# Four stacked graph layers on one core: first stage by groups of blocks, node numbers and spike state in PSUM, 64 early scatters

## The chip, the cores and the metric

The program runs on one core of one Trainium2 chip. The metric is the device time of one execution in microseconds (us). Engines are named as in the profile: PE is TensorE (PEld its weight loads), DVE is VectorE, ACT is ScalarE, POOL is GpSimd, SP is SyncE, which only issues DMAs here. A node graph of 6250 nodes, padded to 49 blocks of 128, has 106250 edges, padded to 832 tiles of 128.

## The reference

```python
x = x + L0(relu(layernorm(x)))      # x: [6250, 128]
x = x + L1(relu(layernorm(x)))
x = x + L2(relu(layernorm(x)))
x = x + L3(relu(layernorm(x)))
# L0, hyperbolic: two Moebius steps (product with weight.T, addition of a fixed bias
#   point), log map, sum over edges src->dst, exp map, relu of the log map, exp map
def mobius_add(x, y):
    x2, y2, xy = sum(x*x), sum(y*y), sum(x*y)
    return ((1 + 2*xy + y2)*x + (1 - x2)*y) / max(1 + 2*xy + x2*y2, MIN_NORM)
# L1, graph attention with 4 heads (softmax over a node's edges), then 25 steps of
def step(mem):                       # a spiking neuron on every element of h
    mem = 0.9*mem + h
    spk = mem > 1.0
    return mem - spk, spk            # result: spikes / 25
# L2: for each of 4 edge types, sums over edges in both directions, times matrices
# L3: two graph convolutions with edge weights, layer norms between
```

## The kernel before

All of x, and most of what is made from it, stays in SBUF as 49 blocks of 128 nodes (`X`, `H`, `T`, `ACC`, 128 x 6272 and a little more). `GB = 7` blocks are a group, `NG = 7` groups are all.

**A walk** sums over edges. The rows of the source nodes lie in a table in DRAM. POOL runs through the 832 tiles of edges and issues one indirect DMA for each (L619): it gathers the table's rows for 128 edges into `GATHERED`. Four tiles are a chunk, 208 chunks are a walk, and `GATHERED` is a ring of four chunks. For each chunk DVE makes a one-hot matrix of destinations: `IOTA` (the numbers of a block's 128 nodes, int16) compared with a column of destinations, `DSTF` (L1309, 128 x 512, a `tensor_tensor` with `is_equal`), PE multiplies it with the gathered rows (L730), and DVE adds the product to the block's sum (L1332). Chunks that touch a second block do this again. DVE then frees the chunk's place in the ring (L1371, a semaphore that POOL waits for). There are six such passes over the edges with gathers: l0, g1 (attention; without one-hots on DVE), l2, l2b, l3a, l3b. l3a and l3b make their one-hots as four `tensor_scalar` instructions with weights (L1315). A seventh pass, gb, reads back by SP's DMAs what g1 has gathered.

**Beside walk l0** DVE sorts the edges by source block. In the first half `count` compares `BUCKET` with a number (L1488, `SAME`) and adds up (L1497), in the second `rank` does for 50 buckets: `SAME` (L1488), a scan `BEFORE` over `ONE` and `SAME` (L1535), `BEFORE * SAME` (L1538), `PLACEF + BEFORE` (L1540). All lie in `EX` in SBUF, 832 columns each. The places are used by 832 **scatters** (L632, indirect DMAs of POOL into `list_dram`): `EARLY = 96` of them after walk l0, the next 336 after walk g1, and the last 400 after gb. POOL's queue is in this order: walk l0, 96 scatters, wait for the stored table `gat_tab`, walk g1, 336 scatters, wait for the end of gb, 400 scatters, wait for the stored `typed_tab`, walk l2, walk l2b, l3a, l3b.

**Before walk l0** (the first stage) SP loads everything, with x near the end; DVE waits for all 39 loads (L1138), turns the edge lists into columns, makes the weights ready, and then works on all 49 blocks at once: layer norm, a dense product group by group (`dense`, `copy_dense`), and the formulas of L0 as 128 x 6272 passes with small 128 x 49 computations between. DVE asks ACT for square roots, logarithms and so on (`ask`), and waits for each answer. One DMA stores `T` as `row_tab0` (L512), and POOL's walk waits for it.

**After walk l0** the rest of L0 is done in the same manner, and then a layer norm by groups: `norm_groups` runs `center`, `variance` and `normed` of DVE for group after group, shifted against each other by one step, while ACT squares and PE multiplies, and SP stores `gat_tab` in seven pieces (`store_groups("l1", ...)`, `n_out`).

**The spikes** (L1766 to L1787): for each group 25 steps on 128 x 896 elements in two halves. DVE computes `MEM = -0.9 * NEG + cur` (L1776) and `NEG = (MEM > 1) - MEM` (L1780), each as two instructions of 448 columns, all in SBUF; ACT makes spikes of `MEM` (L1074, L1045), PE adds them up in PSUM. `typed_beside` does layer 2's norm and products for the group before between the steps.

The kernel's instructions are all written in one function, `program`.

Of the kernel before, what the change touches and what calls it, by code (L numbers as in the profile page):

```python
# [28 lines left out]
F32 = mybir.dt.float32  # L29
# [7 lines left out]
P = 128  # L37
# [25 lines left out]
def program(nc, x, src, dst, etype, weight, w0, b0, w1, att_src, att_dst, b1,  # L63
# [37 lines left out]
    EARLY = 6 * BATCH  # L101
    MIDDLE = EARLY + 21 * BATCH
# [18 lines left out]
    with ctx:  # L121
# [34 lines left out]
        DST2 = SM[:, 0:NT]  # L156
# [19 lines left out]
        W0T = sb("W0T", [P, D])  # L176
# [14 lines left out]
        RI = T[0:RP, 0:3 * RK * P].bitcast(I32)  # L191
        RF = H[0:RP, 0:4 * RK * P]
        RSZ = RK * P
        R16 = H[0:RP, 4 * RK * P:5 * RK * P].bitcast(I16)
        SAME, BEFORE, PLACEF, BUCKET = (EX[:, k * NT:(k + 1) * NT] for k in range(4))
# [12 lines left out]
        WLIN = T[:, 3 * RSZ:3 * RSZ + 2 * NT4 * D]  # L208
        W0N = EQ[:, 3 * D:4 * D]
        RANGEF = T[0:1, 4 * RSZ:4 * RSZ + 4 * NCH]  # L210

        s_in = sem("s_in")
        s_pad = sem("s_pad")
# [71 lines left out]
        class Dense:  # L285
            def __init__(self, n, product=True):
                self.stage = sem(f"dense_stage_{n}")
                self.tr = sem(f"dense_tr_{n}")
                if product:
                    self.ht = sem(f"dense_ht_{n}")  # L290
                    self.mm = sem(f"dense_mm_{n}")
                self.out = sem(f"dense_out_{n}")
# [7 lines left out]
        denses = {"l0": 0}  # L300
        norms = {n: k for k, n in enumerate(("l1", "l2", "l3a", "l3b", "out"))}
# [4 lines left out]
        N_LOADS = 39  # L306
# [59 lines left out]

        def small(k):
            return SM[:, k * NB:(k + 1) * NB]

        STAGE = G[:, 0:GB * D]  # L370
# [41 lines left out]
        def runs_bank(h):  # L412
# [6 lines left out]
        NEG = ACC[:, 2 * GB * D:3 * GB * D]  # L419
# [3 lines left out]
        TURNED, NODE_TERM = (PS[:, 1024 * k:1024 * k + GB * D] for k in (1, 2))  # L423
# [3 lines left out]
        SQ_T = (H[:, 0:NB * D], T[:, 0:NB * D], ACT.Square)  # L427
        requests = {
            "before_l0": [SQ_T,
                          (small(0), small(1), ACT.Sqrt),  # L430
                          (T[:, 0:NB * D], H[:, 0:NB * D], ACT.Square),
                          (small(2), small(3), ACT.Sqrt),
                          (SMALL[:, 41:42], SMALL[:, 40:41], ACT.Sqrt),
                          (SMALL[:, 43:44], SMALL[:, 42:43], ACT.Tanh)],
            "l0": [(H[:, 0:NB * D], T[:, 0:NB * D], ACT.Square),
# [21 lines left out]
        def _(sp):  # L457
# [4 lines left out]
            def load(dst_, src_):  # L462
                sp.dma_start(dst_, src_).then_inc(s_in, 16)
# [1390 lines left out]
```

## Time and profile before

| | us |
|---|---|
| three runs | 8385.81, 8386.53, 8389.94 |
| median | 8386.53 |
| the profiled execution | 8386.38 |
| its span in the trace | 8384.7 |
| DVE busy | 3407.2 (41%) |
| PE busy | 3380.2 (40%) |
| POOL busy | 5866.1 (70%) |
| ACT busy | 1148.5 (14%) |

The span is the time from the first to the last instruction in the trace; the profiled execution lasted 1.7 us longer than it. The prediction's sum is made against 8386.4. In rows of a timeline the first number is the start in us, the second the duration, and `x2` says that two instructions are merged; a row's bracket has the idle time before it and what ended it.

### The profile page before, as it was taken

Reading aid. Unit: us, or ns where it says so; the run is one execution under the profiler, and the core shown is the slowest. Engines: PE = TensorE matmul, PEld = TensorE weight load, DVE = VectorE, ACT = ScalarE, POOL = GpSimd, SP = SyncE. Lnnn points to the kernel's source line nnn. Section 1 sums busy time; section 2 is a strip of 40 time slices with the busy share of each in tenths; the row PEclk is TensorE's granted clock in tenths of the full one; section 3 lists DMA queues with packets and bytes.
Section 4 is the critical chain, followed back from the end, with each engine's and each line's share of the span. In section 5 each row is a group of like instructions: output and inputs, shape, how many; then the busy total and the mean of one; then the engine's idle time right before and its main releaser. Section 6 shows DMA issues by size and latency. Waiting matters only on the chain.

```text
span 8384.7 us, 80823 instructions
## 1 busy us (share of the span) xinstructions
PE 3380.2 (40%) x13790; PEld 2554.1 (30%) x13791; DVE 3407.2 (41%) x7346; ACT 1148.5 (14%) x1948; POOL 5866.1 (70%) x5837
## 2 busy tenths in 40 slices
PE   1344443100002665442555543333345544455553
PEld 1244332100002555111444431111134444344442
DVE  4434656300004556992323323333343333433335
ACT  1000001333331111772000000000010000100001
POOL 0577777777777751787777777777757777477774
PEclk7555555555555666565555555555555555555555
DMA  1112111355553332001222222222222121111111
GB/s 39 52 51 50 45 46 33 92 135 135 135 135 84 87 86 67 19 27 39 70 70 70 69 65 77 77 76 77 76 54 52 52 53 52 48 52 53 52 52 47
DMA packets 348608, 555.47 MB, mean 66 GB/s; under 512 B 121171, under 2 KB 200871, under 8 KB 348511
## 3 DMA queue, kind: packets, MB, share of 16 engines
q0 software_dynamic: 199680, 357.35, 17.7%
q1 hardware_dynamic: 148831, 197.20, 7.8%
q14 instruction: 82, 0.67, 0.0%
q8 instruction: 15, 0.25, 0.0%
HBM read 448.57 MB, written 105.56 MB: 66 GB/s over the span
## 4 chain that ended last, share of the span: by engine, by line
POOL 41%; issue 21%; PE 16%; DVE 10%; DMA 7%; DVEq 4%; ACT 1%; SPq 0%; ACTq 0%; POOLq 0%
POOL GATHERED L619 34%; PE PS L730 15%; POOL list_dram L632 7%; DVE OH L1315 2%; DMA GATHERED<-row_tab,SRCI 2%; DMA GATHERED<-typed_b_tab,PLACE 2%; DVEq L317 1%; DVE OH L1309 1%; DMA GATHERED<-gat_tab,SRCI 1%; DVE T L1120 1%; DVE SM L1130 1%; DMA gat_rows<-GATHERED 1%; DMA GATHERED<-typed_tab,KEYF 1%; DVEq L319 1%; DVE T L1705 1%
## 5 line engine op out<-in xcount | busy, mean ns | idle before, releaser
L730 PE MATMUL PS<-GATHERED,OH 128*128 128x128 f32 (+2 forms) x9216 | 2434.1, 441 | 3059.1 <-DVE OH L1309 688.3
L619 POOL DMA_INDIRECT GATHERED<-row_tab,SRCI x2496 | 2466.4, 988 | 1157.8 <-issue 688.1
L730 PEld LDWEIGHTS PS<-GATHERED,OH 128*128 128x128 f32 (+1 forms) x9216 | 1899.7, 300 | 3651.7 <-issue 2182.7
L632 POOL DMA_INDIRECT list_dram<-REC,PLACE x832 | 973.8, 1170 | 507.7 <-issue 261.5
L619 POOL DMA_INDIRECT GATHERED<-typed_b_tab,PLACE x832 | 816.0, 981 | 261.7 <-issue 224.8
L619 POOL DMA_INDIRECT GATHERED<-typed_tab,KEYF x832 | 818.1, 983 | 253.6 <-issue 241.1
L619 POOL DMA_INDIRECT GATHERED<-gat_tab,SRCI x832 | 785.0, 943 | 253.6 <-issue 222.8
L1315 DVE TENSOR_SCALAR OH<-IOTA,DSTF,WF 128x128 f32 x2048 | 581.5, 360 | 433.3 <-issue 406.9
L1332 DVE TENSOR_TENSOR T<-T,PS 128x128 f32 x512 | 146.8, 287 | 962.7 <-PE PS L730 961.2
L730 PE MATMUL PS<-T,OH 128*128 128x132 f32 x2048 | 426.6, 382 | 241.2 <-DVE OH L1309 141.1
L730 PEld LDWEIGHTS PS<-T,OH 128*128 128x128 f32 x2048 | 383.1, 280 | 284.7 <-issue 193.2
L787 PE MATMUL PS<-AMP,EQ 128*128 x832 | 60.3, 177 | 977.4 <-DVE EX L1622 962.5
L1309 DVE TENSOR_TENSOR OH<-IOTA,DSTF 128x512 f32 (+1 forms) x512 | 353.8, 691 | 136.4 <-issue 123.4
L1332 DVE TENSOR_TENSOR ACC<-ACC,PS 128x129 f32 (+1 forms) x512 | 147.9, 289 | 624.4 <-PE PS L730 623.6
L1332 DVE TENSOR_TENSOR X<-X,PS 128x128 f32 x256 | 73.7, 288 | 714.0 <-PE PS L730 713.8
L787 PEld LDWEIGHTS PS<-AMP,EQ 128*128 128x128 bf16 x832 | 38.4, 107 | 998.6 <-issue 998.6
L928 ACT ACTIVATE H<-T,DINV 128x128 f32<-128x128 f32 x98 | 29.9, 394 | 2103.7 <-DVEq L1825 2103.7
L1622 DVE TENSOR_REDUCE EX<-PS 128x48 f32 x208 | 43.2, 208 | 674.3 <-DMA gat_rows<-GATHERED 489.9
L1335 DVE TENSOR_REDUCE EQ<-PS 128x128 f32<-128x384 f32 x256 | 142.7, 557 | 425.0 <-PE PS L730 425.0
L1309 DVE TENSOR_TENSOR OH<-IOTA,REC 128x512 bf16 (+1 forms) x256 | 177.7, 694 | 215.2 <-issue 213.1
L866 PE MATMUL PS<-ACC,WSB 128*128 128x448 bf16 x350 | 145.0, 514 | 283.1 <-ACT ACC L1045 283.1
L1002 ACT ACTIVATE SCR<-ROWI,SM 128x512 bf16<-128x512 int16 x208 | 150.0, 721 | 670.8 <-DMA ROWI<-dst_rows 667.8
(268 smaller groups left out, 3415.0 us busy)
## 6 DMA issues: line engine op xcount, KB each, us to landing
gat_rows<-GATHERED SPq DMA_DIRECT2D x208, 264.0 KB, 2.3
GATHERED<-gat_rows SPq DMA_DIRECT2D x208, 264.0 KB
GATHERED<-row_tab,SRCI POOLq DMA_INDIRECT x2496, 2.5
ROWI<-dst_rows SPq DMA_DIRECT2D x208, 128.0 KB
typed_b_tab<-ACC SPq DMA_DIRECT2D x49, 384.0 KB, 2.4
list_dram<-REC,PLACE POOLq DMA_INDIRECT x832
GATHERED<-gat_tab,SRCI POOLq DMA_INDIRECT x832
GATHERED<-typed_tab,KEYF POOLq DMA_INDIRECT x832, 2.5
```

The costliest lines, as they stand in the source:

```text
L317: eng.load(regs[p], table[0:1, bass.ds(c * REGS, REGS)])
L319: eng.reg_alu(counts[p][k], regs[p][k], 0, ALU.max)
L619: pool.indirect_dma_start(out=rows_at[:, u * CT + t, 0:width], out_offset=None, in_=table, in_offset=bass.IndirectOffsetOnAxis(ap=rows[:, ...
L632: pool.indirect_dma_start(out=list_dram, out_offset=bass.IndirectOffsetOnAxis(ap=PLACE[:, t:t + 1], axis=0), in_=REC[:, 2 * t:2 * t + 2], ...
L730: last = mm(bank(p)[:, 0:r.shape[1]], onehot(p, t, 1, onehots_), r, start=(t == 0), stop=(t == CT - 1))
L787: last = mm(bank(k)[:, t * AW:(t + 1) * AW], onehots_[:, t * P:(t + 1) * P], AMP[:, bass.ds(b * AW, AW)], start=True, stop=True)
L866: last = mm(SPIKES[:, k, :], IDB, SPK[t % 2][:, k * (GB * D // 2):(k + 1) * (GB * D // 2)], start=(t == 0), stop=(t == LIF_T - 1))
L1002: nc.scalar.activation(SCRB[:, CE:2 * CE], ROWI[:, u * CE:(u + 1) * CE], ACT.Abs, bias=NODE[:, bass.ds(first, 1)], scale=float(FAR)).then_ ...
L1309: return v.tensor_tensor(onehot(p, 0, CT, of).rearrange("p (t w) -> p t w", t=CT), IOTA[:, bass.ds(b * P, P)].rearrange("p (o w) -> p o w" ...
L1315: last = v.tensor_scalar(onehot(p, t), IOTA[:, bass.ds(b * P, P)], DSTF[:, bass.ds(c * CT + t, 1)], weights[:, bass.ds(c * CT + t, 1)], AL ...
L1332: return v.tensor_tensor(dest, dest, bank(p)[:, 0:F], ALU.add)
L1335: return v.tensor_reduce(JOINED[k], bank(p)[:, 0:NP3 * F].rearrange("p (i f) -> p f i", i=NP3), axis=AX.X, op=ALU.add)
```

## The change

1. **First stage by groups.** W0, the bias b0 and x are loaded first, x in two parts (blocks 0 to 20, then the rest), each with its own semaphore. The norm and the product of L0 run through `norm_groups("l0", ...)` with a fourth part, `squared`, five steps late. ACT takes the products out of PSUM, and their squares. The product gets a 129th column, `W0T` times the bias point, so that the dot products with the bias come from PE; the norms of the input rows come from PE too (`HN2`). The length of the Moebius sum is worked out from the small numbers instead of by passes over all blocks. Edge lists, chunk ends and weights are made ready between the small computations (`post()` in place of `ask()`, `answered()` later), some of it on ACT. `T` is finished and stored in seven groups; ACT makes the 49 blocks of bias rows. The zeroing of `ACC` moves to POOL.
2. **Node numbers in PSUM.** The column that one-hots are compared with is now `COLUMN`, in PSUM, copied there for each walk; `SAME` and `PLACEF` are in PSUM too.
3. **64 early scatters** instead of 96; 368 after g1 instead of 336; the last 400 as before.
4. **Spikes.** `NEG` is in PSUM. The `memset` and the first step's `MEM` are left out (the first membrane value is `cur`), and the last step's `NEG`.

```diff
-    EARLY = 6 * BATCH
-    MIDDLE = EARLY + 21 * BATCH
+    EARLY = 4 * BATCH
+    MIDDLE = EARLY + 23 * BATCH
-        SAME, BEFORE, PLACEF, BUCKET = (EX[:, k * NT:(k + 1) * NT] for k in range(4))
+        BLOCK_OF, BEFORE, BUCKET = (EX[:, k * NT:(k + 1) * NT] for k in range(3))
+        PLACEF, COLUMN, SAME = (PS[:, 1024 * k:1024 * k + NT] for k in (1, 2, 3))
-        NEG = ACC[:, 2 * GB * D:3 * GB * D]
+        NEG = [PS[:, 2048 + 512 * h:2048 + 512 * h + HALF] for h in range(2)]
...
@@ SP
+            load(W0N, w0, s_first)
+            bcast(YROW, b0.rearrange("a b -> (a b)"), s_first)
+            for k, b0_ in enumerate(X_PARTS):                       # X_PARTS = (0, 3)
+                a, b = b0_ * GB, (X_PARTS[k + 1] * GB if k + 1 < len(X_PARTS) else NB - 1)
+                load(X3[:, a:b, :], x[a * P:b * P, :].rearrange("(b p) f -> p b f", p=P), s_x[k])
...
-            sp.dma_start(row_tabs[0].rearrange("(b p) f -> p b f", p=P), T3).then_inc(s_stored, 16)
+            for g in range(NG):
+                sp.wait_ge(s_tab, g + 1)
+                sp.dma_start(row_tabs[0][g * GB * P:(g + 1) * GB * P, :].rearrange("(b p) f -> p b f", p=P),
+                             group(T3, g)).then_inc(s_stored, 16)
@@ POOL
+            pool.wait_ge(s_pair, 1)
+            pool.wait_ge(s_wt, 3)
+            pool.memset(ACC[:, :], 0.0).then_inc(s_zero, 1)
-            pool.wait_ge(s_stored, 16)
+            pool.wait_ge(s_stored, 16 * NG)
             walk("l0", row_tabs[0], D, SRCI)
@@ ACT
+            def product_rows(g):
+                columns_out(g, D + 1, 0, D, T3, ACT.Copy)
+                columns_out(g, D + 1, 0, D, H3, ACT.Square)
+                return columns_out(g, D + 1, D, D + 1, small(20).rearrange("p (b o) -> p b o", o=1), ACT.Copy)
+            norm_groups("l0", product_rows, squares=True)
...
+            act.wait_ge(s_h, 2)
+            for g in range(NG):
+                for b in range(g * GB, (g + 1) * GB):
+                    last = nc.scalar.activation(H3[:, b, :], YROW, ACT.Copy, scale=small(22)[:, b:b + 1])
+                last.then_inc(n_biased, 1)
@@ DVE
+            norm_groups("l0", X3, arrivals=X_PARTS, squares=5)
+            post()
+            edge_rows()
+            answered()
+            dve.sem_inc(s_rows, 1)
+            post()
+            ts(small(2), small(2), MIN_NORM, None, ALU.max)
+            chunk_ends()
+            answered()
...
-            tt(H3, T3, over(YROW, NB), ALU.mult)
-            total(xy, H3)
...
-            tt(T3, T3, spread(small(21)), ALU.mult)
-            tt(H3, over(YROW, NB), spread(small(22)), ALU.mult)
-            tt(T3, T3, H3, ALU.add)
-            ask()
-            total(small(5), H3)
-            ask()
+            (seven 128 x 49 operations)
+            post()
+            source_blocks()
+            answered()
...
+            dve.sem_inc(s_h, 1)
+            for g in range(NG):
+                tt(group(T3, g), group(T3, g), spread(group_of(21, g)), ALU.mult)
+                dve.wait_ge(n_biased, g + 1)
+                tt(group(T3, g), group(T3, g), group(H3, g), ALU.add)
+                dve.sem_inc(s_tab, 1)
...
-                                           column[:, bass.ds(c * CT, CT)]...
+                                           COLUMN[:, bass.ds(c * CT, CT)]...
...
-                v.memset(NEG, 0.0).then_inc(lif, 1)
                 for t in range(LIF_T):
+                    mem = MEM[t % 2] if t else cur
+                    if t:
+                        (two MEM halves, from NEG[h] in PSUM and half(cur, h))
+                    if t < LIF_T - 1:
+                        (two NEG halves, out=NEG[h] in PSUM, in0=half(mem, h), in1=half(mem, h))
```

The lines in round brackets stand for instructions told above.

## Rows read from the trace of the kernel before

**Rows 1.** The chain of work that ended last, its shares by engine.
```profile
POOL 41%; issue 21%; PE 16%; DVE 10%; DMA 7%; DVEq 4%; ACT 1%; SPq 0%; ACTq 0%; POOLq 0%
```

**Rows 2.** Busy time by stage: window, its length, engines' busy time (instructions), PE clock, DMA share, GB/s.
```profile
0.00:265.90 265.90, 40.77 (x245) 37.82 (x246) 145.92 (x168) 46.40 (x36) 6.92 (x14) 0.67 0.17 43
265.90:1409.60 1143.70, 525.64 (x2044) 457.25 (x2044) 575.60 (x855) 43.22 (x207) 889.28 (x832) 0.50 0.18 48
1409.60:1559.90 150.30, 27.17 (x169) 23.77 (x167) 93.92 (x117) 47.13 (x72) 120.74 (x98) 0.59 0.12 29
1559.90:2598.40 1038.50, 72.56 (x1012) 46.66 (x1012) 99.01 (x510) 363.46 (x504) 784.97 (x832) 0.50 0.56 134
2598.40:3320.10 721.70, 439.69 (x2118) 394.04 (x2118) 434.36 (x769) 111.24 (x260) 369.49 (x336) 0.67 0.30 79
3320.10:3929.90 609.80, 219.92 (x595) 76.87 (x595) 466.89 (x795) 364.26 (x422) 483.63 (x400) 0.60 0.08 22
3929.90:5001.40 1071.50, 574.71 (x2187) 451.63 (x2187) 316.81 (x607) 83.27 (x195) 818.07 (x832) 0.57 0.25 70
5001.40:6079.10 1077.70, 374.07 (x1028) 112.22 (x1028) 395.20 (x768) 0.00 (x0) 815.96 (x832) 0.50 0.28 76
6079.10:7176.50 1097.40, 543.61 (x2191) 468.81 (x2191) 396.50 (x1331) 26.38 (x70) 787.89 (x832) 0.55 0.20 53
```

**Rows 3.** Timeline of walk l0 in its second half, DVE and POOL.
```profile
1005.95 0.65 DVE L1488 TENSOR_SCALAR EX<-EX,KCOL 128x832 f32<-128x832 f32 x1 [0.24 <-issue]
1006.75 1.95 DVE L1535 TENSOR_TENSOR_SCAN EX<-ONE,H,EX 128x832 f32<-128x832 f32 x1
1007.03 2.42 POOL L619 DMA_INDIRECT GATHERED<-row_tab,SRCI  x1 [0.30 <-issue]
1009.76 0.94 POOL L619 DMA_INDIRECT GATHERED<-row_tab,SRCI  x1 [0.30 <-issue]
```

**Rows 4.** Timeline of the spikes.
```profile
3349.45 1.30 POOL L632 DMA_INDIRECT list_dram<-REC,PLACE  x1 [0.30 <-issue]
...
3350.90 1.15 DVE L1776 SCALAR_TENSOR_TENSOR ACC<-ACC,T 128x448 f32<-128x448 f32 x2
3351.06 1.30 POOL L632 DMA_INDIRECT list_dram<-REC,PLACE  x1 [0.31 <-issue]
```

**Rows 5.** Groups of instructions, shapes apart: busy us, mean ns of one, idle before.
```profile
L1309 DVE TENSOR_TENSOR OH<-IOTA,DSTF 128x512 f32 x504 | 348.3, 691 | 131.4 <-issue 119.6
...
L1807 DVE TENSOR_TENSOR ACC<-PS,ACC 128x512 f32<-128x512 f32 x49 | 33.9, 692 | 9.3 <-issue 9.3
L928 ACT ACTIVATE H<-T,DINV 128x128 f32<-128x128 f32 x98 | 29.9, 394 | 2103.7 <-DVEq L1825 2103.7
```

**Rows 6.** Timeline after walk l0: norm by groups, the 64th scatter, and SP past the stores.
```profile
1500.76 1.09 DVE L1130 TENSOR_REDUCE SM<-X 128x7 f32<-128x896 f32 x1
...
1506.24 1.09 DVE L1130 TENSOR_REDUCE SM<-X 128x7 f32<-128x896 f32 x1
...
1511.08 1.33 POOL L632 DMA_INDIRECT list_dram<-REC,PLACE  x1 [0.30 <-issue]
...
1528.07 0.35 SPq L533 DMA_DIRECT2D ACC<-dst_rows  x1
```

**Rows 7.** Timeline of the first stage: the load of x, the table's store, the first gather.
```profile
14.60 16.14 SPq L463 DMA_DIRECT2D X<-in_x  x2
...
253.09 0.39 SPq L512 DMA_DIRECT2D row_tab<-T  x1
...
265.89 1.11 POOL L619 DMA_INDIRECT GATHERED<-row_tab,SRCI  x1 [258.32 <-DMA row_tab<-T]
```

**Rows 8.** Busy time in pieces of the first stage, columns as in rows 2.
```profile
48.60:85.00 36.40, 17.81 (x98) 17.03 (x98) 20.08 (x34) 0.00 (x0) 0.00 (x0) 0.77 0.04 6
...
178.60:188.80 10.20, 0.00 (x0) 0.00 (x0) 8.08 (x35) 3.29 (x5) 0.00 (x0) 0.50 0.00 0
...
202.20:205.20 3.00, 0.00 (x0) 0.00 (x0) 2.61 (x12) 0.00 (x0) 0.00 (x0) 0.50 0.00 0
...
238.00:246.30 8.30, 0.00 (x0) 0.00 (x0) 6.89 (x31) 1.50 (x2) 0.00 (x0) 0.50 0.00 0
```

More of the change, by code:

```diff
@@ L299, in program @@
         typed_mm = sem("typed_mm")
-        denses = {"l0": 0}
-        norms = {n: k for k, n in enumerate(("l1", "l2", "l3a", "l3b", "out"))}
+        norms = {n: k for k, n in enumerate(("l0", "l1", "l2", "l3a", "l3b", "out"))}
         stores = {"l3a": 1, "l3b": 2}
@@ new lines, in edge_columns, with columns, cols @@
+            def edge_columns():
+                def columns(a):
+                    return PS[:, 1024 * a:1024 * (a + 1)].rearrange("p (b f) -> p b f", b=2)[:, :, 0:4 * RP]
+                def cols(t):
+                    return t[:, :].rearrange("p (b f) -> p b f", b=2)
+                dve.wait_ge(s_const, 9)
+                dve.wait_ge(s_cols, 1)
+                step(v.tensor_copy(cols(SRCF), columns(0)))
+                step(v.tensor_copy(cols(DSTF), columns(1)))
+                step(v.tensor_copy(cols(KEYF), columns(2)))
+                step(v.tensor_copy(cols(WF), columns(3)))
+                dve.sem_inc(s_wc, 1)
@@ new lines, in source_blocks @@
+            def source_blocks():
+                step(v.tensor_copy(SRCI[:, :], SRCF[:, :]))
+                dve.sem_inc(walks["l0"].free, RING)
+                step(v.tensor_copy(BLOCK_OF.bitcast(I32), SRCF[:, :]))
+                step(v.tensor_single_scalar(BEFORE.bitcast(I32), BLOCK_OF.bitcast(I32), 7, ALU.logical_shift_right))
+                step(v.tensor_copy(BUCKET, BEFORE.bitcast(I32)))
+                dve.wait_ge(s_drow, 64)
+                chunk_table(RANGEF, RANGES)
+                dve.sem_inc(s_info, 1)
@@ L1266, in normed, with squared @@
                     dve.sem_inc(n_normed, 1)
-                for s in range(NG + 2):
-                    for part, g in ((center, s), (variance, s - 1), (normed, s - 2)):
-                        if 0 <= g < NG:
-                            part(g)
+                def squared(g):
+                    dve.wait_ge(n_out, k * NG + g + 1)
+                    total(small(squares)[:, g * GB:(g + 1) * GB], group(H3, g))
+                parts = [(center, 0), (variance, 1), (normed, 2)] + ([(squared, 5)] if squares else [])
+                for s in range(NG + parts[-1][1]):
+                    for part, late in parts:
+                        if 0 <= s - late < NG:
+                            part(s - late)
             def artanh(o, n):
@@ L1322, in all_added, with aggregate @@
                 hold(dve, wk.more_added, before + more + 1)
-            def aggregate(name, result, F, weights=None, ahead=None, column=DSTF, table=RANGES,
+            def aggregate(name, result, F, weights=None, ahead=None, table=RANGES,
                           parts=((NIT - 1, None, None),), sets=2, joins=False):
@@ L1699, in _ @@
             dve.sem_inc(v_made, RING)
+            step(v.tensor_copy(COLUMN, DSTF[:, :]))
             wk = walks["gb"]
@@ L1796, in _ @@
             stt(other, DSTF[:, :], 1.0, other, ALU.add, ALU.mult)
-            tt(DST2, DSTF[:, :], other, ALU.subtract)
+            tt(COLUMN, DSTF[:, :], other, ALU.subtract)
             for s in (nb_turned, nb_ht, nb_mm, nb_made, nb_high, nb_rest, nb_middle):
```

482 lines of the change are left out of this document (219 added, 263 removed).

## Prediction

> **What bounds the kernel now.** I read the chain of waits first. Its largest shares are POOL with 41% and "issue" with 21%, ahead of PE with 16% [rows 1]; "issue" is mostly the 0.30 us that lie between two of POOL's DMA instructions. Then I cut the span into stages, a window for each item of POOL's queue [rows 2]. Nine windows say what sets each stage. In a walk nothing is waited for but POOL: walk g1 takes 1038.5 us for 832 gathers, 1.248 us each, of which 784.97 / 832 = 0.943 us busy. Walk l3a, whose one-hots are made by `tensor_scalar`, keeps that busy time (787.89 / 832 = 0.947). But l0 has 889.28 / 832 = 1.069, l2 983 ns and l2b 981 ns, all for the same instruction.
>
> The timelines say why. While DVE runs the scan L1535 (1.95 us, operands `ONE` and `SAME`, both in SBUF), a gather takes 2.42 us, and the next one 0.94 [rows 3]. In the spikes, where DVE issues instructions with two SBUF tensors back to back, every scatter takes 1.30 us (0.97 elsewhere) and starts 1.61 us after the one before, three times the 0.535 us between two starts of DVE [rows 4]. So POOL waits for the DVE instruction in progress to end when that instruction reads two tensors from SBUF. I compared every POOL duration with what DVE ran beside it: instructions that read one of their two tensors from PSUM (L1332, L1807) left it at 0.94. DVE itself is not slowed, with 691 ns for every one-hot [rows 5].
>
> **The change part by part.**
>
> *Walks.* With `COLUMN` in PSUM a one-hot has one SBUF tensor; so have the scan, the product and the sum of `rank`. L1488 wrote `SAME` in SBUF in 0.65 us; into PSUM I take 1.02, the time of the other passes over 832 columns, since 0.65 is too short for a column a cycle. In a pair of chunks of the ranking half (10.0 us after the change) DVE then has some 7.6 us of work, still under POOL. Walk l0: 1143.7 - 832 x 1.249 = 104.5, less 4 for the passes half-way that still read `SRCF` and `DSTF`: **-101**. Walk l2: 1071.5 - 1040 - 5.5 for L1811, which keeps two SBUF operands: **-26**. l2b: 1077.7, of which 8.7 is the wait before it, minus 1041 and 3 for L1340: **-25**. g1, l3a, l3b: 0. The copies into `COLUMN` add 1 us each before gb and l2b: **+2**.
>
> *Price of PSUM.* L1807 reads one tensor from PSUM and takes 692 ns for 512 columns against 691 for L1309 [rows 5]: nothing added. No row shows DVE writing to PSUM or reading there with a step of zero; nearest are the same rows, so I take 0 and bound it by double time, below, as a rival. The Trainium skill (VectorE: DVE Perf Modes, section on the TRN2 errata) gives 62 cycles more for a PSUM source than for an SBUF one, an estimate of 65 ns each; in gb, where one-hots are on the path, its 256 would add 17 us. The two rows disagree with it, so the sum leaves it out.
>
> *Early scatters.* The window after walk l0 is 150.3 us long because 96 scatters are [rows 2]. The table that g1 needs was stored at 1528.07, where SP's next DMA starts, 118.5 us after the walk; the 64th scatter began at 1511.08 and was done 16 us before [rows 6]. So the store is what ends last with 64: **-32**. With 96, g1 could gain nothing from a faster norm; with 64 the cover is 16 us. The 32 moved scatters cost 32 x 1.4 = 45 us after g1, where POOL is idle for 246 of 721.7 us [rows 2]: 0.
>
> *Last 400 scatters.* This stage is POOL's: 483.63 us busy and 400 x 0.31 between them leave nothing of its 609.8, while the spikes were done at 3808 and the last typed table was under way to DRAM by 3834 [rows 2]. 400 x 1.27 would be 508; some 70 of the 100 us lie beside L1776 and L1780, the rest beside passes that stay. L1776 now reads `NEG` from PSUM; L1780 still reads `MEM` twice. Of a period of 2.14 us half is then free of waiting. I follow three scatters: one starts free, the next (1.27 later) waits 0.335 for the end of the first NEG half, the third 0.135 for the second: 0.16 on average against 0.335. **-37**. Between -10 (POOL is held by every pair anyway) and -72 (no waits left). The operations left out, 2 us a group, are hidden.
>
> *First stage*, 265.9 us now [rows 7]. New, step by step. (a) x was issued in 16.14 us for 49 blocks; 21 blocks from 3.5 on, 7 us, and 2.5 to land: DVE starts at 13, by when the bias work (5 us of small instructions, after 6) is done. (b) `norm_groups`: the same code later has a step of 5.48 us, DVE being full [rows 6]; `squared` adds 1.12, so 6.6 from the fifth step; 2.5 + 3.8 + 3 x 5.4 + 2 x 6.6 + 3.8 + 2.5 = 42 us up to the last `normed`, and 12 until the last group's transposes, product, squares and sums (8 in that later stage, and two more ACT passes): 67. (c) Small computations that stay: 10.2 + 3.0 + 8.3 = 21.5 [rows 8]. Seven new ones, 1.7. Edge and chunk work, now between them: 17.6, most of it from the piece between 48.6 and 85.0, where DVE was busy for 20.08 us [rows 8]; the copies of the weights in that piece go to ACT. 67 + 21.5 + 1.7 + 17.6 = 108. (d) Bias rows: 49 x 0.394 = 19.3 us on ACT [rows 5], longer than DVE's 15.5 beside them, and a last sum: 128.5. (e) The last group's store lands in 3 to 3.6 instead of the 12.5 of the whole table [rows 7]: 132. POOL's zeroing of `ACC` and the weights on PE and ACT lie beside (c) with little to spare. **-134**, between -110 (each hand-over and ACT's copies late, PE at its lower clock throughout) and -145.
>
> Sum: -134 - 101 - 32 - 37 - 26 - 25 + 2 = -353. From 8386.4, the profiled execution's time, that is **8033**; the median of the three runs is 0.1 higher.
>
> **The rivals.**
>
> *A. The stretch of gathers doesn't come from two SBUF operands.* Then walks and late scatters stay, and -134 - 32 + 2 give 8222. For it: nothing in the rows; it would need another reason why l3a is clean. The Trainium skill (SBUF — State Buffer, section "Who interferes with whom") says that `tensor_tensor` takes only the shared read interface and, as an inference, that making a DMA's descriptors needs the write interface, so it would not hold it up; by that rule this is the outcome. The 2.42 us gather beside the scan speaks against the rule.
>
> *B. PSUM is slow for DVE.* The only way to a slower kernel. It is one price, time per column in the changed instructions. If it doubles, a one-hot costs 0.53 more, which in gb, where DVE and PE take turns, is 256 x 0.53 = +137; a spike half costs 0.47 more, 672 of them move the spikes' end from 3811 to 4127 on the old clock, 234 beyond POOL's new end at 3893. +371 against -353: about 8404, and the point where it turns is 95% of a doubling. L1807 and L1332 show no such price.
>
> *C. The first stage gives about 100 only*, because ACT, with five passes a group, a PE at its lower clock and the weights' chain (PE, ACT, PE, ACT) fall behind DVE: 8067. For it: 12 hand-overs in (b) and (c) that I priced by busy time.
>
> *D. The spikes' scatters stay locked* to DVE's pairs: -10 in place of -37, 8060.
>
> *E. Waits vanish beside L1780 too* (one tensor read twice), and the first stage is at its best: -35 and -11 more, 7987.
>
> **How the numbers follow.** Forecast 0.60, C 0.14, D 0.10, E 0.08, A 0.05, B 0.03. The forecast's own range, with the first stage at 125 to 145 and the scatters at 25 to 50, is 8009 to 8056. The range that should hold 8 in 10 reaches past C and D together to 8090 and nearly to E, 7990. A measurement of this kernel can tell about 0.2%, 17 us, from no change. All cases but B are faster by far more: faster 0.96, same 0.01, slower 0.03.
>
> **What would show it.** First gather near 132 us; walk l0 1043 us long, its gathers at 0.945 us also beside the scans; POOL idle some 15 us before g1, which starts 118 us after walk l0; scatters beside the spikes at 1.1 us on average; l2 and l2b at 0.95 us a gather; L1309 at 691 ns. The prediction is wrong if one-hots or L1780 are longer than now, if the first stage ends past 160, or if DVE's chunks in the ranking half become later than POOL's.

## The result

| | median | runs | from to |
|---|---|---|---|
| before | 8388.2 us | 4 | 8385.8 to 8390.7 |
| after | 8077.6 us | 4 | 8073.6 to 8090.7 |

The ratio is 0.963, with a 95% interval from 0.962 to 0.965: 311 us less, 3.7%. The forecast was 8033, its wide range 7990 to 8090, the forecast's own range 8009 to 8056. The profiled execution of the changed kernel took 8090.7 us (span 8088.9), 13 more than the median and the longest of the four. The steps below are compared with that execution, as the forecast's sum was made against the profiled one of before.

The windows by stage, cut at the same events as in [rows 2] (columns: stretch, its length, then busy time and count of PE, PEld, DVE, ACT and POOL, granted TensorE clock, DMA share, GB/s):

```profile
0.00:146.60 146.60, 61.99 (x343) 58.77 (x344) 105.67 (x213) 60.83 (x140) 12.50 (x14) 0.71 0.29 78
146.60:1225.20 1078.60, 511.24 (x2028) 451.32 (x2028) 612.10 (x844) 43.20 (x207) 786.61 (x832) 0.53 0.20 51
1225.20:1352.00 126.80, 30.72 (x171) 27.32 (x171) 94.52 (x120) 41.47 (x64) 81.16 (x64) 0.61 0.11 28
1352.00:2391.30 1039.30, 73.12 (x1024) 49.58 (x1024) 106.96 (x519) 369.23 (x512) 785.87 (x832) 0.50 0.55 134
2391.30:3121.80 730.50, 443.17 (x2118) 397.89 (x2118) 434.22 (x770) 111.22 (x260) 385.96 (x368) 0.66 0.30 78
3121.80:3690.60 568.80, 219.08 (x595) 76.84 (x595) 445.06 (x760) 364.23 (x422) 443.02 (x400) 0.61 0.08 24
3690.60:4735.80 1045.20, 575.26 (x2187) 452.93 (x2187) 314.40 (x607) 83.25 (x195) 791.76 (x832) 0.57 0.25 71
4735.80:5785.10 1049.30, 374.12 (x1028) 112.23 (x1028) 393.06 (x770) 0.00 (x0) 786.73 (x832) 0.50 0.29 78
```

Against [rows 2], stage by stage (the last stage is what remains of the two spans; the forecast's +2 for copies stands as +1 before gb and +1 in l2b):

| stage | forecast | measured |
|---|---|---|
| up to the first gather | -134 | -119.3 |
| walk l0 | -101 | -65.1 |
| early scatters, up to g1 | -32 | -23.5 |
| walk g1 | 0 | +0.8 |
| from g1 to the end of gb | +1 | +8.8 |
| last 400 scatters | -37 | -41.0 |
| l2 | -26 | -26.3 |
| l2b with its wait | -24 | -28.4 |
| l3a, l3b and the end | 0 | -1.7 |
| sum | -353 | -295.7 |

In the chain of waits POOL has fallen from 41% to 32%, and PE has risen from 16% to 20% [rows 1]:

```profile
POOL 32%; issue 21%; PE 20%; DVE 15%; DMA 6%; DVEq 5%; ACT 1%; SPq 0%; ACTq 0%; POOLq 0%
```

Two misses can be read from the trace at once. The first is in the ranking half of walk l0 (timeline; columns: start, length, engine, line, operation, idle time before it and what ended it):

```profile
1009.35 1.09 DVE L1499 TENSOR_SCALAR PS<-EX,KCOL 128x832 f32<-128x832 f32 x1 [0.22 <-issue]
1010.46 0.94 POOL L628 DMA_INDIRECT GATHERED<-row_tab,SRCI  x1 [0.30 <-issue]
1010.58 1.95 DVE L1546 TENSOR_TENSOR_SCAN EX<-ONE,H,PS 128x832 f32<-128x832 f32 x1
1011.71 0.94 POOL L628 DMA_INDIRECT GATHERED<-row_tab,SRCI  x1 [0.30 <-issue]
1012.56 1.02 DVE L1549 TENSOR_TENSOR EX<-EX,PS 128x832 f32<-128x832 f32 x1
...
1013.62 1.03 DVE L1551 TENSOR_TENSOR PS<-PS,EX 128x832 f32<-128x832 f32 x1
1014.21 0.94 POOL L628 DMA_INDIRECT GATHERED<-row_tab,SRCI  x1 [0.30 <-issue]
1014.56 0.68 DVE L1300 TENSOR_TENSOR OH<-IOTA,PS 128x512 f32 x1
...
1016.09 2.09 PE L736 MATMUL PS<-GATHERED,OH 128*128 128x129 f32 x8 [5.60 <-DVE OH L1300]
...
1018.32 0.29 DVE L1323 TENSOR_TENSOR ACC<-ACC,PS 128x129 f32 x1 [2.29 <-PE PS L736]
1018.80 0.94 POOL L628 DMA_INDIRECT GATHERED<-row_tab,SRCI  x1 [2.40 <-DVEq L1362]
```

The gathers beside the scan take 0.94 us, where one took 2.42 [rows 3]. But then POOL idles 2.40 us for a free buffer: four ranking operations stand one behind the other, the next chunk's one-hot comes only after them, PE has waited 5.60 us for it, and its sums (2.09 us) come after that.

The second miss is in the first stage. POOL zeroes `ACC` there, and one small cast of DVE, 0.34 us otherwise, lasts as long as that:

```profile
111.17 5.54 POOL L619 MEMSET ACC<- 128x6468 f32 x1 [103.28 <-PE PS L724]
146.62 1.10 POOL L628 DMA_INDIRECT GATHERED<-row_tab,SRCI  x1 [29.91 <-DMA row_tab<-T]
```

```profile
111.32 5.59 DVE L1170 CAST RANGES<-PLACE 1x208 int32<-1x208 f32 x1
```

### The profile page after: what moved, and what is told of

It reads as the page before. It is cut to its first block, busy times and chain, and to the rows that moved or that the text cites. A ratio compares the mean times of both kernels' runs of the same rounds, so it can differ in the third digit from the quotient of the medians.

```text
span 8088.9 us, 81271 instructions
## 1 busy us (share of the span) xinstructions
PE 3395.1 (42%) x13888; PEld 2581.8 (32%) x13889; DVE 3385.8 (42%) x7359; ACT 1163.0 (14%) x2052; POOL 5650.1 (70%) x5838
## 4 chain that ended last, share of the span: by engine, by line
POOL 32%; issue 21%; PE 20%; DVE 15%; DMA 6%; DVEq 5%; ACT 1%; SPq 0%; ACTq 0%; POOLq 0%
POOL GATHERED L628 27%; PE PS L736 19%; POOL list_dram L641 5%; DVE OH L1306 3%; DVE OH L1300 2%; DMA GATHERED<-row_tab,SRCI 2%; DVEq L321 2%; DMA GATHERED<-typed_b_tab,PLACE 2%; DVE T L1141 1%; DVE EX L1546 1%; DVE SM L1151 1%; DVE EQ L1326 1%; DVEq L323 1%; DMA GATHERED<-gat_tab,SRCI 1%; DVE PS L1499 1%
## 5 line engine op out<-in xcount | busy, mean ns | idle before, releaser
L628 POOL DMA_INDIRECT GATHERED<-row_tab,SRCI x2496 | 2363.1, 947 | 965.6 <-issue 677.2
L641 POOL DMA_INDIRECT list_dram<-REC,PLACE x832 | 910.1, 1094 | 490.4 <-issue 262.2
L628 POOL DMA_INDIRECT GATHERED<-typed_b_tab,PLACE x832 | 786.8, 946 | 262.6 <-issue 219.9
L628 POOL DMA_INDIRECT GATHERED<-typed_tab,KEYF x832 | 791.8, 952 | 253.6 <-issue 239.2
L1300 DVE TENSOR_TENSOR OH<-IOTA,PS 128x512 f32 (+3 forms) x1024 | 702.8, 686 | 493.2 <-issue 471.3
L915 ACT ACTIVATE H<-T,DINV 128x128 f32<-128x128 f32 x98 | 29.9, 394 | 2103.6 <-DVEq L1841 2103.6
L927 ACT ACTIVATE H<-T 128x896 f32<-128x896 f32 x35 | 33.8, 966 | 1171.9 <-DVEq L1247 1171.9
```

Source lines behind the costliest of these rows:

```text
L628: pool.indirect_dma_start(out=rows_at[:, u * CT + t, 0:width], out_offset=None, in_=table, in_offset=bass.IndirectOffsetOnAxis(ap=rows[:, ...
L641: pool.indirect_dma_start(out=list_dram, out_offset=bass.IndirectOffsetOnAxis(ap=PLACE[:, t:t + 1], axis=0), in_=REC[:, 2 * t:2 * t + 2], ...
L1300: return v.tensor_tensor(onehot(p, 0, CT, of).rearrange("p (t w) -> p t w", t=CT), IOTA[:, bass.ds(b * P, P)].rearrange("p (o w) -> p o w" ...
```

## The experiments

Twelve runs of nine kernels, in three groups, each group on one chip. On the first and the third chip the kernel before was some 18% slower, 9891 and 9939 us (8386 on the second), and the split kernel below 26%, 10121 us against 8048. Those chips have a section of their own. Their total times can't be set beside 8078; lengths of single instructions can, since the gathers there take 0.94 us as well.

### Ranking split over two chunks: e1_split_rank, e1b_split_rank

```diff
             def rank(j, u):
+                k = bucket(j, u)
                 if u % 2 == 0:
-                    k = bucket(j, u)
                     ... # comparison, scan
+                else:
                     ... # product, sum
```

> Same work as the changed kernel; of the four operations that rank a bucket the first two (comparison, scan) stay beside the even chunk and the last two (product, addition) move beside the odd chunk. Theory: in the second half of the first walk a pair of chunks takes 10.36 us on average in place of POOL's 9.98, because 5.1 us of ranking stand in one chunk ahead of VectorE's next one-hot, so that TensorE's sums come late. Then the walk falls from 1078.6 to about 1045 us (1040 to 1055), POOL's gaps between gathers in its second half go, and the run's time falls by 25 to 40 us (about 8040). Rival: VectorE's and TensorE's chain is too long in every chunk, whatever the order of the ranking (PSUM writes, the lower TensorE clock): then the walk stays at 1070 to 1085 and the time within 8 us of the changed kernel's.

On the first chip: 10120.9 us (10090.5 to 10124.4), ratio to the kernel before there 1.022 (1.020 to 1.024). It says nothing on the split: walk l0 took 1324 us, 285 of them in which POOL stood idle. The same kernel on the second chip:

> The same kernel as e1_split_rank, on another occasion: there transfers landed up to 10 us late in every kernel, the kernel before among them (9891 us), and hid what was to be compared. Theory as before: walk l0 falls from 1078.6 to about 1045 us (1040 to 1055), the run by 25 to 40 us, to about 8040. Rival as before: VectorE's and TensorE's chain is too long in every chunk, the walk stays at 1070 to 1085, the time within 8 us of the changed kernel's.

Measured: 8048.1 us (8044.9 to 8057.3), ratio 0.960 (0.958 to 0.961), 29 us below the changed kernel by the medians. (The profiled executions lie 46 us apart, 8044.9 and 8090.7: this one is the shortest of its four, that one the longest.) Walk l0 took 1042.3 us in place of 1078.5, which e6_neg_sbuf and e8_one_hn2, with the walk unchanged, repeat to 0.1. POOL's waits in its ranking half, from 700 us to the walk's end (columns: who waited for whom, us in all, times, longest), first in the changed kernel, then in this one:

```profile
POOL GATHERED L628 <- issue: 108.2, 355, 0.3
POOL GATHERED L628 <- DVEq L1362: 45.9, 39, 2.6
```

```profile
POOL GATHERED L628 <- issue: 112.1, 368, 0.3
POOL GATHERED L628 <- DVEq L1362: 7.0, 23, 0.3
```

Of 45.9 us of waits for a free buffer 39 are gone; what is left is 0.3 us each, the idle time that stands before every gather. The same operations were done, with the same lengths (1.09, 1.95, 1.02, 1.03), so the rival falls: it was their place, not their price. The stage behind the walk shrank as well, from 126.8 to 120.2 us, because DVE no longer has chunks left over when POOL is done:

```profile
1188.20:1308.40 120.20, 29.86 (x171) 26.53 (x171) 90.66 (x112) 41.47 (x64) 81.97 (x64) 0.63 0.11 29
```

### Zeroing by ScalarE: e2_zero_by_act

```diff
-            pool.wait_ge(s_pair, 1)
-            pool.wait_ge(s_wt, 3)
-            pool.memset(ACC[:, :], 0.0).then_inc(s_zero, 1)
...
@@ ACT, behind its copies of the weights
+            act.wait_ge(s_pair, 1)
+            act.wait_ge(s_const, 9)
+            for k in range(2):
+                last = nc.scalar.activation(ACC[:, k * (NB * XW // 2):(k + 1) * (NB * XW // 2)],
+                                            IOTA[:, 0:NB * XW // 2], ACT.Copy, scale=0.0)
+            last.then_inc(s_zero, 1)
```

> The zeroing of ACC (128x6468) moves from one POOL memset to two ScalarE copies of finite numbers with scale 0. Theory: POOL's memset holds back VectorE's cast (5.59 us in place of 0.34), so the cast takes 0.34 again, and the first gather starts 5 us sooner, at about 141.3 instead of 146.6. Rival 1: ScalarE's two copies (estimate from 0.92 us for 896 elements: 6.5 us) come past the time when VectorE waits for the logarithm, and the gain is eaten: first gather at 145 to 148. Rival 2: the long cast had another cause and stays at 5.6 us.

The time, 10079.4 us on the first chip, says nothing; the first stage does:

```profile
107.88 0.34 DVE L1171 CAST RANGES<-PLACE 1x208 int32<-1x208 f32 x1
108.25 0.34 DVE L1172 CAST RANGES<-PLACE 1x208 int32<-1x208 f32 x1
108.79 5.70 ACT L985 ACTIVATE ACC<-IOTA 128x3234 f32<-128x3234 int16 x2
139.33 1.10 POOL L624 DMA_INDIRECT GATHERED<-row_tab,SRCI  x1 [131.45 <-DMA row_tab<-T]
```

No cast is long any more, and the first gather starts at 139.3. The three kernels with this edit start it at 139.3, 140.4 and 141.1 us, the other runs, e8_one_hn2 apart, nine with the changed kernel, between 142.3 and 151.2. Most of that spread comes before the zeroing: DVE's last sum of the norm ends between 74.3 and 83.2 us, in kernels that are alike up to there. From that end to the first gather it is 68.0 to 68.1 us in the nine, and 63.8, 64.1 and 64.1 in the three. So the edit is worth 4 us, less than the 5.25 that the cast gets back: at the logarithm DVE now waits 1.05 us for ACT, whose answer comes behind the zeroing. Rival 1 came in this small part.

### The column back in SBUF: e3_column_sbuf, e3b_column_sbuf

```diff
-        PLACEF, COLUMN, SAME = (PS[:, 1024 * k:1024 * k + NT] for k in (1, 2, 3))
+        PLACEF, SAME = (PS[:, 1024 * k:1024 * k + NT] for k in (1, 3))
+        COLUMN = sb("COLUMN", [P, NT])[:, :]
```

> The changed kernel with the column of node numbers, which the plain one-hots compare, back in SBUF, in a tile of its own; all else as changed. Theory (VectorE operations with two SBUF operands hold back POOL's gathers, those with one operand in PSUM do not): the walks l2 and l2b grow again by 25 us each (20 to 30), the counting half of the first walk by 10 to 20, the walk gb, which POOL does not bound, by 0 to 5: together 60 to 80 us, 8140 to 8155. Rival (the walks l2 and l2b gained from something else in the change): 0, within 10 us of the changed kernel.

> The same kernel as e3_column_sbuf, of which the first look came from a chip that delayed every kernel's transfers; the gathers there took 25 and 22 us more in l2 and l2b and 17 more in l0 than in e1_split_rank beside it. Theory: l2 and l2b longer by 22 to 27 us each than the changed kernel's 1045.0 and 1039.9, l0 by 5 to 17: 8077 + 60 = about 8137 (8125 to 8150). Rival (the walks' gain came from something else): within 10 us of the changed kernel.

Both runs fell on the chips with pauses: 10039.3 us (10001 to 10068) and 10108.7 (10106 to 10129). The forecast of 8137 is untested. The gathers' lengths answer the question all the same. Groups of POOL's instructions, walk l2b, in this kernel and in e1_split_rank beside it on the same chip (columns: count, busy time and mean ns of one, idle before it):

```profile
L629 POOL DMA_INDIRECT GATHERED<-typed_b_tab,PLACE x832 | 810.5, 974 | 401.3 <-issue 244.7
```

```profile
L628 POOL DMA_INDIRECT GATHERED<-typed_b_tab,PLACE x832 | 786.9, 946 | 442.6 <-issue 237.2
```

974 ns with the column in SBUF, 946 with it in PSUM: 23.6 us of the 29 that l2b had gained (981 ns before). Nothing else differs between the two in this walk. In l0 the gathers' time over 0.96 us is 18.9 and 20.2 us in the two runs, 1.5 to 1.7 in kernels with column and `SAME` in PSUM. In l2 it is 31 and 28 against 4 to 19, less clean, since other work of DVE lies beside it.

### The comparison's result back in SBUF: e4_same_sbuf, e4b_same_sbuf

```diff
-        PLACEF, COLUMN, SAME = (PS[:, 1024 * k:1024 * k + NT] for k in (1, 2, 3))
+        PLACEF, COLUMN = (PS[:, 1024 * k:1024 * k + NT] for k in (1, 2))
+        SAME = EX[:, 3 * NT:4 * NT]
```

> The changed kernel with SAME (the comparison's result, which the scan and the product read) back in SBUF. Theory: the comparison takes 0.65 again in place of 1.09 us, but the gathers beside the scan take about 2.4 us again, and those beside the product are late too, in 50 buckets: the first walk goes from 1078.6 to 1110 to 1140, the time up by 30 to 60 us. Rival (the gathers' delay does not come from two SBUF operands): the gathers stay at 0.94, VectorE's part of a bucket is 0.44 us shorter, and the walk falls by up to 22 us, to 1057 to 1078.

> The same kernel as e4_same_sbuf, from an undisturbed chip. There 50 gathers beside scan and product took 1.10 us more each. Theory: a pair of chunks of the ranking half then takes POOL 9.98 + 1.10 = 11.1 us in place of the 10.36 that VectorE and TensorE make of it now, 50 pairs: walk l0 up by 35 to 45 us, to about 1118, the run at about 8117. Rival (the scan's operands don't matter, and the walk only gains VectorE's 0.44 us a bucket): walk 1057 to 1078, run 8055 to 8077.

Again both on the chips with pauses: 10053.2 us (9992 to 10058) and 10132.5 (10080 to 10145); the times of the walk can't be had. The timeline of the first:

```profile
1099.61 0.65 DVE L1500 TENSOR_SCALAR EX<-EX,KCOL 128x832 f32<-128x832 f32 x1 [0.19 <-issue]
1100.40 1.95 DVE L1547 TENSOR_TENSOR_SCAN EX<-ONE,H,EX 128x832 f32<-128x832 f32 x1
1100.84 2.26 POOL L629 DMA_INDIRECT GATHERED<-row_tab,SRCI  x1 [0.31 <-issue]
1102.39 1.03 DVE L1550 TENSOR_TENSOR EX<-EX 128x832 f32<-128x832 f32 x1
1103.41 0.94 POOL L629 DMA_INDIRECT GATHERED<-row_tab,SRCI  x1 [0.30 <-issue]
```

The stretched gather is back. 50 gathers beside scan and product last 1.10 us longer each, 55 us in all; in the kernel before the same count gives 50 and 1.10. The rival that two SBUF operands don't matter falls with this run.

### Three edits together: e7_all_three

The split, the zeroing by ScalarE, and

```diff
-        PLACEF, COLUMN, SAME = (PS[:, 1024 * k:1024 * k + NT] for k in (1, 2, 3))
+        PLACEF, COLUMN, STARTED = (PS[:, 1024 * k:1024 * k + NT] for k in (1, 2, 3))
+        ONEP = PS[:, 3072 + NT:3072 + NT + 1]
+        SAME = EX[:, 3 * NT:4 * NT]
...
-                    v.tensor_tensor_scan(BEFORE, ONE[:, :].to_broadcast([P, NT]), SAME, ...
+                    v.tensor_tensor_scan(STARTED, ONEP.to_broadcast([P, NT]), SAME, ...
...
-                    v.tensor_tensor(BEFORE, BEFORE, SAME, ALU.mult)
+                    v.tensor_tensor(BEFORE, STARTED, SAME, ALU.mult)
```

> The changed kernel with three edits: ranking split over two chunks as in e1_split_rank; ACC zeroed by ScalarE as in e2_zero_by_act; SAME in SBUF, where the comparison takes 0.65 us instead of 1.09, while the scan reads its ones and writes its result in PSUM, so that scan, product and addition still have one operand in PSUM. Theory: first gather 5 to 7 us sooner (about 140), walk l0 at 1043 (1038 to 1050) with POOL's gathers at 0.94 throughout, the tail behind it 2 to 5 us shorter: 8077 - 6 - 35 - 3 = about 8033 (8020 to 8045). Rival 1 (the scan's contention comes from what it writes or from SAME, not from its count of SBUF operands): gathers beside the scan take 2.4 us again and the walk stays at 1075 or more. Rival 2 (only POOL's rate counts once the ranking is split): nothing beyond the split and the 6 us, which gives the same 8035 to 8040, and the faster comparison is worth nothing by itself.

Measured: 8051.8 us (8049.8 to 8065.1), ratio 0.960 (0.959 to 0.962), no better than the split alone, and above the expected 8020 to 8045. The first gather came at 140.4, as expected, but walk l0 took 1055.5 us, 13 more than in e1b_split_rank. The gathers by row_tab (three walks), here and there:

```profile
L626 POOL DMA_INDIRECT GATHERED<-row_tab,SRCI x2496 | 2378.9, 953 | 1030.1 <-issue 674.8 <-DMA row_tab<-T 269.6 <-DVEq L1366 85.8
```

```profile
L628 POOL DMA_INDIRECT GATHERED<-row_tab,SRCI x2496 | 2364.0, 947 | 931.0 <-issue 685.4 <-DMA row_tab<-T 168.9 <-DVEq L1362 76.8
```

They are busy 14.9 us longer. Put down by what DVE ran beside each, 12.4 us of it lie on 75 gathers (by groups 0.10 to 0.21 each) beside the comparison at 0.65 us, which has only one SBUF tensor to read; beside the scan alone nothing is lost. So a comparison from SBUF to SBUF, at the faster rate, also holds POOL, here in both halves of the walk. That the zeroing by ScalarE is not the reason is seen in e2_zero_by_act and e9_split_and_zero, whose gathers in l0 lose 1.7 and 1.5 us only. Writing the comparison to PSUM costs DVE 0.44 us and frees POOL, and with the split DVE has the time to spare. Neither rival had this; the expectation was wrong by 13 us of walk.

This agrees with the Trainium skill (SBUF — State Buffer, section "Who interferes with whom"), which says that `tensor_scalar` in a mode that uses both of DVE's SBUF ports blocks GpSimd; here 0.65 us for 832 columns against 1.09 into PSUM shows the faster mode.

### The spikes' state in SBUF: e6_neg_sbuf

```diff
-        NEG = [PS[:, 2048 + 512 * h:2048 + 512 * h + HALF] for h in range(2)]
+        NEG = [ACC[:, 2 * GB * D + HALF * h:2 * GB * D + HALF * (h + 1)] for h in range(2)]
```

> The changed kernel with NEG, the spikes' state that two operations a step pass on, back in SBUF. Theory (scatters wait for VectorE operations with two SBUF operands): 220 scatters beside the spikes had a mean of 0.153 us over 0.96; with NEG in SBUF both operations of a step have two SBUF operands again, the mean excess goes to 0.3 or more, and the stage of the late scatters grows from 568.8 by 15 to 40 us. Rival (the 41 us came from 32 more scatters moved and fewer operations a step, not from PSUM): the stage stays within 8 us.

Measured: 8107.1 us. The stage of the late scatters, POOL's busy time in the fifth column of work:

```profile
3097.10:3703.40 606.30, 222.09 (x595) 78.17 (x595) 446.43 (x760) 364.47 (x422) 480.81 (x400) 0.59 0.08 22
```

606.3 against 568.8 us, all of it POOL's busy time (480.8 against 443.0), so 37.5 of the 41.0 us come from this one operand. The other 3.5 remain for all else, the operations left out among it. The time of the whole, one run, lies only 30 us above the changed kernel's median, since the stage before, where nothing was changed, was 20 us shorter in it (see "From g1 to the end of gb" below).

### One sum of squares in place of seven: e8_one_hn2

```diff
-                        for t in range(GB):
-                            last = mm(HN2[:, g * GB + t:g * GB + t + 1], HTSQ[:, t * P:(t + 1) * P], ONE[:, :],
-                                      start=True, stop=True)
+                        last = mm(HN2[:, g * GB:(g + 1) * GB], HTSQ[:, 0:P], ONE[:, :].to_broadcast([P, GB]),
+                                  start=True, stop=True)
```

> The changed kernel in whose first normalisation the squared norms of the rows are summed by one TensorE product of a group's first block in place of seven (the other six blocks' norms are left out, that is, take the first one's). Theory: the chain of a group on TensorE (7 transposes 1.74 us, product 3.4, norm sums 1.9) and ScalarE's copies between them bound the pipeline's tail, 7 to 7.7 us a group, so that VectorE is done at 78.6 instead of 67; with one sum the group falls to some 5.7 us and the first stage's end comes 6 to 10 us sooner. Rival (ScalarE's passes bound it): less than 2 us.

Measured: 8072.0 us in its one run, 5.6 below the changed kernel's median and close to its shortest run (8073.6), so the time of the whole shows no clear gain. The first stage does: first gather at 131.6 in place of 146.6. The chain of waits of the changed kernel in the tail of the norm, one group:

```profile
60.99 1.61 PE PS L676 x7
62.60 0.02 issue
62.62 0.93 ACT ROWI L937
63.55 0.04 issue
63.59 3.38 PE PS L683 x14
66.97 1.68 PE PS L687 x14
68.65 0.84 PE PS L676 x7
```

This group takes 7.66 us, every step of it on PE but the one copy; the six from group to group take 6.8 to 8.8, 7.5 on average. PE in the timeline of the experiment, last group:

```profile
55.92 0.96 PE L676 MATMUL PS<-IDENT,H 128*128 128x128 f32 x7
57.89 1.83 PE L683 MATMUL PS<-W0X,ROWI 128*128 128x129 f32 x14 [1.01 <-ACT ROWI L936]
59.55 0.28 PE L686 MATMUL PS<-ONE,ACC 128*128 128x7 f32 x2
```

Some 4 us; the six from group to group take 3.8 to 6.6, 5.4 on average. The gain of 15 us is larger than the 6 to 10 expected, because products fell too. The product of a group takes 3.0 to 3.4 us in all seven groups of the changed kernel; beside all but the first the granted clock was 0.50 to 0.56, that is 1.2 GHz for most or all of it. (The first takes 3.38 in both kernels, at a granted 1.00; why is open.) Four of the seven here take 1.83 us, within stretches granted 2.4 GHz, and the whole stage has 0.76 against 0.71. Whether the lighter load brought the clock, or chance, isn't shown. Against the nine runs whose norm is unchanged (first gather 142.3 to 151.2) the gain is 11 to 20 us. So PE's chain held the first stage, and the sums of squares, 14 matmul passes for 7 columns, were the part of it that could be moved.

### More early scatters, and the split with the zeroing: e5_early96, e9_split_and_zero

```diff
-    EARLY = 4 * BATCH
-    MIDDLE = EARLY + 23 * BATCH
+    EARLY = 6 * BATCH
+    MIDDLE = EARLY + 21 * BATCH
```

> The changed kernel with 96 early scatters in place of 64, 32 fewer beside the walk gb. Theory: 64 scatters end at 1326.4, POOL is then idle for 25.6 us until the table of g1 is stored, at 1352.0; 32 more at 1.25 to 1.55 us are 40 to 50 us, so g1 starts 15 to 25 us later, and the 32 scatters fewer in the stage of gb give nothing back, since TensorE bounds it: 8092 to 8102. Rival 1 (the table is late with the scatters too): no loss, 8077. Rival 2 (fewer scatters in gb's stage shorten it): the stage from g1's end to gb's end falls by 5 us or more.

> The changed kernel with two edits, the ranking split over two chunks and ACC zeroed by ScalarE; SAME stays in PSUM. Theory: walk l0 at 1042 us as in e1b_split_rank, with no excess of the gathers (e7_all_three lost 13 us to its 0.65 us comparison from SBUF to SBUF), first gather 5 us sooner than there: 8048 - 5 = about 8043 (8035 to 8050), the fastest of all. Rival: the 13 us that e7_all_three's walk lost have another cause, the zeroing by ScalarE, and this walk is 1055 too: about 8052.

Both ran on the third chip only: 10114.9 us (10105 to 10140) and 10154.4 (10135 to 10209). From the end of walk l0 to the start of g1 there lie 169.5 us with 96 scatters and, in e9_split_and_zero, 150.4 with 64, but other kernels with 64 have up to 176 on these chips. Whether 64 or 96 is better is open. So is the time of the two edits together: the forecast of 8043 is untested. That the gathers in l0 lose nothing (1.5 us over 0.96) speaks against its rival, and the first gather is at 141.1.

### The chips with pauses

| chip | before | kernels of the change's kind |
|---|---|---|
| first | 9891 | e1 10121, e2 10079, e3 10039, e4 10053 |
| third | 9939 | e5 10115, e9 10154, e3b 10109, e4b 10132 |

All eight are slower than the kernel before, by 1.4% to 2.3%. The instructions are as long as elsewhere, but queues stand still. In e1_split_rank, walk l0:

```profile
313.08 0.69 DVE L1300 TENSOR_TENSOR OH<-IOTA,PS 128x512 f32 x1 [1.52 <-issue]
...
313.91 2.06 PE L736 MATMUL PS<-GATHERED,OH 128*128 128x129 f32 x8 [2.68 <-DVE OH L1300]
...
323.27 0.29 DVE L1323 TENSOR_TENSOR ACC<-ACC,PS 128x129 f32 x1 [9.51 <-remote]
323.78 0.94 POOL L628 DMA_INDIRECT GATHERED<-row_tab,SRCI  x1 [3.61 <-DVEq L1362]
```

PE's sums are done at 316.0, the gathered rows are there, and DVE goes on at 323.3; even the register operation with which its queue computes the value to wait for runs only at 323.1. My guess in the expectation of e1b_split_rank, late transfers, was wrong: ACT used the rows of the next chunks on time, every 5 us. Such a pause comes about once in the four chunks of a turn of the loop: POOL idles at a free buffer every 23 to 27 us, 285 us in the walk. In the spikes, which are straight code, the waits of e5_early96 are longer still:

```profile
PEld PS L871 <- issue: 476.3, 67, 50.0
PE PS L871 <- issue: 369.2, 55, 48.4
```

Where DVE, ACT or PE pause, a stage does not wait for POOL's gathers, and what the change saves there is lost: on the first chip e3 and e4, whose gathers are longer, were even faster than e1 and e2. That accounts for a gain that vanishes, not for a loss of 2%. The stages that grew most in e1_split_rank are the ones that DVE, ACT and PE set: from g1 to the end of gb 1108.9 us in place of 728.1, the late scatters with the wait behind them 827.6 in place of 568.6. No trace of the kernel before from these chips exists, nor a run of the changed kernel itself. What makes the queues pause, and where the kernel before loses less, stays open.

## Why the prediction came out as it did

**The number.** 8077.6 lies in the wide range (7990 to 8090), 45 us above the forecast and outside the range that was given for the case forecast, 8009 to 8056, with a chance of 0.60. It is near rival C's 8067, but not for C's reason alone: the wide range was built from C and D, and D did not come. What filled it were half of C (15 us), a cost in walk l0 and behind it that had no price at all (43 us by e1b_split_rank), and 8 us of a stage whose length varies by itself; parts that gave up to 4 us more than forecast took some of it back. That all this fits into the range is luck in part: the profiled execution, 8090.7, lies at its edge.

**Right, in mechanism and size: two SBUF operands.** The bound of before was read correctly. POOL's gathers wait for DVE instructions with two SBUF tensors, and PSUM takes that away: 2.42 us against 0.94 beside the scan, back to 2.26 with `SAME` in SBUF; 981, 946 and again 974 ns in l2b; -41.0 for the late scatters with a forecast of -37, 37.5 of it by the one operand. 220 scatters beside the spikes have a mean of 0.153 us over 0.96, where the forecast followed three of them to 0.16. l2 (-26.3 against -26) and l2b (-28.4 against -24) hold to 5 us. Rivals A and D fall, and E too: -35 more did not come, and a scatter beside `NEG = (MEM > 1) - MEM`, which reads one SBUF tensor twice, is still long (in the changed kernel's timeline one from 3207.12 us lasts 1.29 us, with L1795 from 3206.96 on). The inference in the Trainium skill behind A (SBUF — State Buffer, "Who interferes with whom": `tensor_tensor` would not hold up descriptor making) is contradicted by e3_column_sbuf, whose one-hots are `tensor_tensor`: 974 ns a gather against 946.

**Right in mechanism, early scatters.** With 64 of them POOL is done at 1326.4 and idle for 25.6 us, until the table is stored: the store ends last, as forecast. The 8.5 us that lack belong to the step below.

**Price of PSUM.** Zero, as taken: one-hots 686 ns (691 before [rows 5]), the sum that writes to PSUM 1.03 us like the product that doesn't. Rival B falls. The 62 cycles of the Trainium skill (VectorE: DVE Perf Modes, TRN2 errata) do not show either, by the estimate from them 65 ns on every one-hot. The comparison took 1.09 us, not 1.02.

**The step that failed: "In a pair of chunks of the ranking half (10.0 us after the change) DVE then has some 7.6 us of work, still under POOL."** The work was nearly right; the step compared busy time with busy time and left out the order. All 5.1 us of ranking stand in one chunk, between the one-hot of a chunk and that of the next, and PE can't start its sums before that one. The wait goes round: DVE, PE (2.09 us), DVE, then POOL's buffer. POOL's gaps come to 38.6 us over 50 pairs, 0.77 us on each pair's 9.98 (the 10.36 in my expectations was too low an estimate). That cost 36 us in the walk, as e1b_split_rank shows by taking it away (1042.3, forecast 1043), and 6.6 of the 8.5 us that the early scatters' stage lacked. The prediction named the case itself in its last sentence, as a sign that it is wrong, without a price; the ring of four buffers does not hide it because it comes back every pair.

**The first stage, -119 in place of -134.** The term of the norm's end was mis-sized: DVE done at 78.6 us, not 67. The last `normed` ended at 59.0 (55 forecast), and what follows took 19.6 us in place of 12, because PE still had two whole groups to do. The chain of a group on PE is 7.5 us on average, 6.8 at the least, where I gave DVE's step of 6.6, and PE's lower clock is part of it; without six of the seven sums of squares DVE was done at 63.6 (e8_one_hn2). Part (c) took 47.1 us in place of 41, 5.3 of it the cast held by POOL's zeroing; "lie beside (c) with little to spare" priced neither engine against the other. Part (d) was 3 us cheaper, 17.6 from the first product to the last sum: ACT needed 14.42 us for its 49 rows, 0.294 each, so DVE set the time. The forecast's 0.394 is what one instruction of L928 lasts, and they overlap: the same row has 29.9 us busy for 98, 0.305 each, which would have given 15 us [rows 5]. Rival C, the first stage at -100, did not come: its reason did, at half its size.

**From g1 to the end of gb, +8.8.** Most likely not the change. The stage's length goes with its granted clock, in six kernels that do nearly the same there: 728 to 733 us at 0.66, 722 at 0.67 (the kernel before, and e7_all_three with the change), and

```profile
2387.10:3097.10 710.00, 424.37 (x2118) 379.08 (x2118) 434.06 (x770) 111.26 (x260) 381.21 (x368) 0.70 0.31 80
```

710 at 0.70, in e6_neg_sbuf, with the changed kernel's instructions. A stage that PE and DVE share thus varies by 20 us with no edit, which the range should have had.

## What to carry to other kernels

When one engine is freed, check the next by its chain, not by its busy time: where in the loop does the long operation stand, and who waits behind it? Spreading the same four operations over two chunks took 36 us from the walk; the change itself had taken 65. If GpSimd issues DMAs, put one operand of every two-tensor VectorE instruction beside it in PSUM, and the result of a `tensor_scalar` at the faster rate as well; and keep GpSimd's own long writes away from stretches where VectorE is on the path. The best version timed is the change with the split ranking, 8048 us, 4.0% under the kernel before; by the parts, the zeroing by ScalarE should take off 4 more (no run on the second chip has these two edits alone), and the sums of squares hold some 15 (11 to 20).

## What the runs showed of the hardware

- DVE writing 832 columns of f32 to PSUM loses the faster rate of a `tensor_scalar` (1.09 us, 0.65 to SBUF) and nothing in two-tensor operations (1.03 us, 1.02).
- A `tensor_scalar` at the faster rate, with one SBUF tensor, holds POOL's DMA instructions too, by 0.1 to 0.2 us on average for those beside it (e7_all_three).
- The block works in both directions: a POOL memset of 5.54 us made a DVE cast of 0.34 us last 5.59.
- The same kernel took 8386 us on one chip and 9891 and 9939 on two others, where queues paused up to 50 us with nothing in the trace that ends the pause; there the order of the kernels was another.
